# Where the first layer of the experts' weights is split into bfloat16 parts

## The reference

```
x = x + ga * attention(layernorm(x) * (1 + ca) + sa)    # 16 heads of 8, rope, causal softmax
x = x + gb * experts(layernorm(x) * (1 + cb) + sb)
# experts: h = x @ Wm + bm is cut into 8 slices of 16 numbers a token; for each slice
w     = softmax(t @ expert_emb)                         # 16 experts, the best 2 are kept
hmid  = gelu(einsum('td,edi->tei', t, W1) + b1)         # 16 -> 64, for every expert
out   = sum over the best 2 of w * (hmid @ W2 + b2)     # then @ Wo + bo
```

## Time and profile before

| | us |
|---|---|
| median of three runs | 404.51 |
| the profiled execution | 403.76 |
| its span in the trace | 402.0 |
| TensorE busy | 339.3 (84%) |
| VectorE busy | 290.0 (72%) |
| ScalarE busy | 256.4 (64%) |
| GpSimd busy | 132.9 (33%) |

### The profile page before, as it was taken

The page is one execution under the profiler, slowest core; times in us unless marked ns, Lnnn a source line. Parts: engine busy times, 40 slices in busy tenths (PEclk is TensorE's granted clock), DMA queues, the critical chain, the costliest instruction groups (busy, mean ns, idle before and its releaser), DMA issues.

```text
span 402.0 us, 7268 instructions
## 1 busy us (share of the span) xinstructions
PE 339.3 (84%) x2637; PEld 158.2 (39%) x2668; DVE 290.0 (72%) x590; ACT 256.4 (64%) x297; POOL 132.9 (33%) x175
## 2 busy tenths in 40 slices
PE   3758688888877899988987899898879898879996
PEld 3424254445543444434553534334444323222123
DVE  5879868898789877875789487874769445972343
ACT  8570443435159878865349878855437997968981
POOL 6345307201421324842313024941410035532500
PEclk9988699999899999999999999999989999999999
DMA  7334214100016055520026255520014355814552
GB/s 258 109 67 71 48 35 66 29 4 0 4 40 98 24 141 138 165 59 3 27 51 98 57 137 135 141 45 4 29 30 50 90 136 142 116 17 122 134 147 70
DMA packets 27115, 31.53 MB, mean 78 GB/s; under 512 B 6780, under 2 KB 17788, under 8 KB 27068
## 3 DMA queue, kind: packets, MB, share of 16 engines
q1 hardware_dynamic: 23372, 28.57, 31.2%
q0 software_dynamic: 3456, 2.39, 2.8%
q10 hardware_dynamic: 252, 0.11, 0.2%
HBM read 3.57 MB, written 1.05 MB: 11 GB/s over the span
## 4 chain that ended last, share of the span: by engine, by line
PE 51%; DVE 21%; issue 10%; ACT 9%; DMA 3%; POOL 2%; SPq 2%; DVEq 0%; ACTq 0%; POOLq 0%
PE misc L1290 17%; PE acc L1290 16%; PE big L1290 16%; DVE mx L1028 8%; ACT ring L769 6%; PE misc L1312 2%; DVE xn L972 2%; DMA block<-qk_turned 1%; DMA tstack<-tp 1%; ACT L802 1%; SPq L492 1%; SPq L517 1%; POOL block L446 1%; DVE stats L947 1%; POOL rpow L591 1%
## 5 line engine op out<-in xcount | busy, mean ns | idle before, releaser
L769 ACT ACTIVATE ring<-big 128x1024 f32<-128x1024 f32 (+2 forms) x225 | 198.2, 929 | 99.7 <-PE big L1290 98.4
L1028 DVE TENSOR_REDUCE mx<-misc 128x1 f32<-128x512 f32 (+7 forms) x155 | 87.8, 588 | 24.2 <-PE misc L1290 22.1
L1290 PE MATMUL acc<-ring,cb 128*32 128x512 f32 x512 | 67.8, 604 | 2.6 <-DVE gm L1148 1.5
L1290 PE MATMUL big<-dense,block 128*128 128x448 bf16 (+7 forms) x249 | 54.3, 318 | 7.4 <-ACT ring L769 7.1
L1290 PE MATMUL big<-tstack,w1s 128*128 128x512 bf16 x178 | 52.4, 381 | 5.6 <-ACT ring L769 3.9
L1290 PE MATMUL misc<-dense,block 128*128 128x320 bf16 (+7 forms) x167 | 42.0, 313 | 8.9 <-DVE mx L1028 8.6
L1148 DVE SCALAR_TENSOR_TENSOR gm<-acc,cb,gm 128x512 f32<-128x512 f32 (+1 forms) x41 | 30.0, 733 | 22.7 <-DMA gm<-wT 12.2
L1290 PEld LDWEIGHTS big<-dense,block 128*128 128x128 bf16 x256 | 30.8, 149 | 33.7 <-ACT ring L769 19.0
L446 POOL DMA_DIRECT2D block<-qk_turned x66 | 39.3, 601 | 7.9 <-DMA tstack<-tp 7.0
L670 POOL TENSOR_TENSOR gm<-osb,gm 128x512 f32<-128x512 f32 x12 | 15.8, 1316 | 76.4 <-ACT osb L809 76.4
L1290 PE MATMUL acc<-ring,vals 128*32 128x64 f32 (+7 forms) x512 | 40.7, 421 | 0.4
(11 more groups left out here) (163 smaller groups left out, 472.0 us busy)
## 6 DMA issues: line engine op xcount, KB each, us to landing
gm<-wT SPq DMA_DIRECT2D x64, 256.0 KB
dense<-qk SPq DMA_DIRECT2D x42, 64.0 KB
tstack<-tp SPq DMA_DIRECT2D x18, 128.0 KB, 4.3
block<-qk_turned POOLq DMA_DIRECT2D x66, 32.0 KB, 3.2
xs<-in_x SPq DMA_DIRECT2D x4, 256.0 KB, 8.1
ca<-in_pack_a SPq DMA_DIRECT2D x1, 769.0 KB, 7.3
out<-lg SPq DMA_DIRECT2D x3, 256.0 KB, 2.3
dense<-tp SPq DMA_DIRECT2D x6, 128.0 KB, 8.9
```

Of the source, the lines that this page charges most:

```text
L769: act.activation(dst, src, func, scale=scale).then_inc(s["ring_read"], 1)
L1028: dve.tensor_reduce(mx[:, g, k:k + n, blk], src, AX.X, ALU.max).then_inc(s["misc_read"], 1)
L1290: return pe.matmul(dst, lhsT, rhs, start=start, stop=stop)
```

## The change

VectorE's four parts are gone, and CUT_AT with them. ScalarE does the two casts, right behind take_gates. GpSimd does what was one scalar_tensor_tensor as two instructions: it multiplies w1p by the row mask into combT (a float32 tensor of 128x1024 that is free until the first experts stage), and adds that to w1f. The first pair stands behind k_blocks(0), the second behind k_blocks(1). ScalarE's second cast waits for GpSimd's first pair (w1_less at 2), GpSimd's pairs wait for the casts (w1_rounded).

```diff
-FOLD_AT, CUT_AT = [12, 15], [18, 21, 24, 27]
+FOLD_AT = [12, 15]
@@ gpsimd
+            def cut_weights(k):
+                pool.wait_ge(s["b_loaded"], 16)
+                pool.wait_ge(s["w1_rounded"], k + 1)
+                less = B["keep"][:, k:k + 1].to_broadcast([P, NE * FI])
+                rounded = combT[:].rearrange("p k t -> p (k t)")
+                pool.tensor_tensor(rounded, w1p, less, ALU.mult).then_inc(s["w1_less"], 1)
+                pool.wait_ge(s["w1_less"], 2 * k + 1)
+                if k:
+                    pool.tensor_tensor(w1s[:, :], rounded, w1f, ALU.add).then_inc(s["w1_ready"], 1)
+                else:
+                    pool.tensor_tensor(w1f, rounded, w1f, ALU.add).then_inc(s["w1_less"], 1)
...
             k_blocks(0, K_BLOCKS)
+            cut_weights(0)
             pool.wait_ge(s["spare_cleared"], 2)
             stack_q(1)
             pool.wait_ge(s["qk_turned"], 6)
             stack_k(1)
             k_blocks(1, K_BLOCKS)
+            cut_weights(1)
@@ scalar
+            def round_weights(k):
+                if k:
+                    act.wait_ge(s["w1_less"], 2)
+                else:
+                    act.wait_ge(s["w1_loaded"], 16)
+                act.copy(w1p, w1f).then_inc(s["w1_rounded"], 1)
...
             take_gates()
+            round_weights(0)
+            round_weights(1)
             act.wait_ge(s["cleared"], 3)
             shift_rows(act, 0, 0, range(1, 2))
             turn(1)
@@ vector
-            def cut_weights(part):
-                dve.wait_ge(s["b_loaded"], 16)
-                dve.wait_ge(s["w1_loaded"], 16)
-                less1, less2 = B["keep"][:, 0:1], B["keep"][:, 1:2]
-                if part == 0:
-                    link(dve.tensor_copy(w1p, w1f))
-                elif part == 1:
-                    link(dve.scalar_tensor_tensor(out=w1f, in0=w1p, scalar=less1, in1=w1f, op0=ALU.mult, op1=ALU.add))
-                elif part == 2:
-                    link(dve.tensor_copy(w1p, w1f))
-                else:
-                    dve.scalar_tensor_tensor(out=w1s[:, :], in0=w1p, scalar=less2, in1=w1f,
-                                             op0=ALU.mult, op1=ALU.add).then_inc(s["w1_ready"], 1)
...
-                if k in CUT_AT:
-                    cut_weights(CUT_AT.index(k))
```

More of the change, by code:

```diff
@@ L354, in build @@
             "gates_filled", "setup_link", "modb_ready", "w1_ready", "summed", "rows_cleared", "tokens_one",
-            "var_ready", "pow_ready", "xn_ready", "out_gates", "expert_gates", "xb_ready", "x1b_ready",
+            "var_ready", "pow_ready", "xn_ready", "out_gates", "w1_rounded", "w1_less", "expert_gates", "xb_ready", "x1b_ready",
             "misc_filled", "misc_read", "ring_filled", "ring_read", "consumed", "acc_read",
```

## The result

| | kernel before | changed kernel |
|---|---|---|
| median of 18 runs, us | 404.88 | 408.23 |
| lowest to highest, us | 401.61 to 406.45 | 404.48 to 409.99 |
| ratio, 95% interval | 1 | 1.0078 (1.005 to 1.0106) |
| profiled execution, us (span) | 403.76 (402.0) | 407.54 (405.7) |

The account below looks back on a forecast made before the run. TensorE and VectorE were taken to pace each other around the edit. +3.15 (VectorE held) - 0.6 (last multiply-add) + 1.0 (clock) = +3.5 us gave 407.3 profiled, 408.0 us as median; range 403.6 to 410.4.

Parts of the forecast that it names:

- VectorE's jobs, 0.6 of 4.1 us on the path: Of four removed VectorE instructions, only the last multiply-add (83.55 to 84.83) delays TensorE; gain about 0.6 us.
- ScalarE's casts free: Casts at 29.1 to 30.1 and until about 42.0 us cost nothing, ending 0.7 us before ScalarE's DMAs at 42.68.
- GpSimd's length, 2.5 us: Each of the four new GpSimd instructions of 128x1024 takes 2.5 us, range 2.2 to 3.3.
- The stall, 3.15 us: GpSimd's second pair, from 67.9 us, holds VectorE's second fold of the gates, which ends 3.15 us later.
- TensorE's idle time, 4.1 us: TensorE waits for maxima behind the second fold, until 74.9 us: 1.00 + 3.15 = 4.1 us.
- The clock, +1.0 us: Granted clock falls 1.4 us into TensorE's new wait, stays low 6.4 us, slowing 3.7 us of work: +1.0 us.
- The sum: Whole kernel: +3.15 held fold, -0.6 last multiply-add gone, +1.0 lower clock, together +3.5 us.
- no meeting: Second fold or GpSimd's second pair lies elsewhere by 2 us: -0.6, 403.9 us; chance 0.12.
- only the first fold instruction is held: In the second fold, GpSimd's addition comes too late to hold more: +1.0 - 0.6, no clock loss, 404.9 us; chance 0.14.
- all 4.1 us come back: VectorE is the bound in 60 to 86 us, so its removed work is fully regained: 401.0 us; chance 0.10.
- the slow GpSimd: GpSimd needs 3.3 us per instruction, delaying ScalarE by 0.9 us and VectorE more: +6.0, 410.5 us; chance 0.10.

Follow-up runs that it names:

- the first experiment: Changed kernel with GpSimd's second pair moved behind stack_q(1), before the wait for element 1's turned queries: 404.16 us, ratio 1.0008 to the kernel before.

## Why the prediction was right

The kind of cause was right: the second pair and the fold of the gates hold each other, TensorE stands still for it, and the clock falls. Which fold is held, and by how much each term weighs, was partly wrong, and the errors nearly cancel.

- *VectorE's jobs, 0.6 of 4.1 us on the path.* Measured 0.56: the distance falls from 3.69 to 3.12 between 76.5 and 88.4. The size is right, its place only in part. By TensorE's instructions 0.16 had come back ahead of the last multiply-add (81.17 and 84.70 are 3.53 apart). At its place TensorE gains 0.75 (85.42 and 88.20, 2.78) and loses 0.36 of that two units later, in the wait of 0.52 before 90.15 (87.01 and 90.15, 3.14). So the jobs counted as free were not quite free, and the wait of 0.59 came back for 0.39.
- *ScalarE's casts free.* They took 1.08 and 1.04 us; the second ended at 41.34 and the DMAs went out at 43.08, 1.7 us later. Right, with more cover than the 0.7 us feared.
- *GpSimd's length, 2.5 us.* The multiplication of bfloat16 took 1.91, the addition 2.36: a pair is 0.7 us shorter than taken. The multiplication passed the bound of 2.2 us from below; it has a bfloat16 input and a broadcast column, which no row had shown, and no run tells which of the two, or the operation itself, makes it shorter.
- *The stall, 3.15 us.* 3.04 us measured (2.69 on L945 and 0.03 on L944 of the first fold, 0.32 on L943 of the second), but not where the step put it. The step failed on the first fold: it took 67.86, the end of the DMA issues, as the moment from which VectorE can be held, and so let L920 (67.09 to 67.78) pass. In the changed kernel GpSimd's last wait ahead of the pair was passed at 67.36, with two DMA issues still to run, and L945, issued at 67.59, was held until the multiplication's end at 70.40. The second fold then came when most of the addition was over, and lost 0.32 us rather than 3.15. That the two agree in sum is partly luck: with the first fold kept clear by a wait, the predicted pattern appears, and holds 2.5 us. The row that would have shown it was in the trace before: L1050, 0.28 us long at its shortest, issued at 169.28 and held until 171.58, while GpSimd's L682 is recorded only from 170.15.
- *TensorE's idle time, 4.1 us.* 3.95 us, but it is another wait: the step added 3.15 to the 1.00 behind the second fold, and measured were 1.22 + 2.73 behind the first. Again the sum agrees by luck.
- *The clock, +1.0 us.* It fell, but not 1.4 us into the wait and for 6.4 us, as the step had it: it fell at the wait's end and stayed low for 3.4 us, all of it behind the wait. The step had come to 3.7 us behind the wait, so this too agrees by luck. That work took longer: TensorE's distance grows from 3.18 (68.43 and 71.61) to 4.36 us (70.33 and 74.68), and then falls back to 3.69. From 71.61 to 76.65 TensorE needed 5.04 us for what took 4.53 from 68.43 to 72.96 before, though the 4.53 contain the second fold's wait of 1.00 us, and only 0.15 is left of it, since the slower TensorE no longer runs ahead of VectorE. The net is +0.5 us. The term was mis-sized: the step gave the full price of slow matmuls and did not take off the wait that they cover.
- *The sum.* +2.73 (growth of the first wait) + 0.51 (from there to 76.65, clock and second fold together) - 0.56 = +2.68 us, against +2.67 by the same instructions at the end of that softmax. The prediction had +3.5. The medians give 3.35 us, 0.7 more than this pair of profiles; what lies between is within the interval of the ratio, and no run here explains it.

Of the rivals, "no meeting" fell with the profile; "only the first fold instruction is held" had the shape nearly right (one instruction carries 2.69 of the 3.04 us) and its price of 1.0 us wrong; "all 4.1 us come back" fell with the first experiment, ratio 1.0008 with the stall removed; the slow GpSimd fell with 1.91 us. What the prediction did not see is that, once the split was gone, the place of the fold was worth more than the split: from 404.16 to 402.28 us, by the profiles 0.56 us gained with the fold in its old place (and no stall) and 1.70 with the late one.

What stays open: whether VectorE is held from the moment that the GpSimd instruction is handed over, or GpSimd's recorded starts are late. Three places show the same 0.8 to 0.9 us between the two (169.28, 67.59, and 68.00 with the pair added). The run with the added wait speaks for the first: there the multiplication cannot have started before 67.40 and is recorded from 67.63, so a recorded start was late by at most 0.23 us. That it was no later at the three places is argued from this one run, not measured there.

## What to carry to other kernels

Moving elementwise work from VectorE to GpSimd gives VectorE back only what was on the path, here 0.6 of 4 us, and it can hold VectorE for the length of the GpSimd instruction: lay the new GpSimd instructions over VectorE's timeline, and keep them beside instructions that were not held, such as reductions out of PSUM. Count from where GpSimd's last wait ahead of the instruction is passed, here 1.0 to 1.3 us before its recorded start, and look again at what GpSimd does next when the order changes. Before moving a job to another engine, try another order of the jobs on its own: here that alone gave a ratio of 0.9971 (0.9946 to 0.9996), with 0.29 us to show for it in the profile, and with the move it gave 0.9954, the best of all.

## What the runs showed of the hardware

- A GpSimd multiplication of 128x1024 with a bfloat16 input and a broadcast mask column took 1.91 us, an addition of two float32 tensors of that size 2.36 us.
- Held beside GpSimd arithmetic: scalar_tensor_tensor on two SBUF tensors (0.69 to 3.38 us), tensor_scalar (0.43 to 2.45), a cast of 32x128 (0.21 to 1.26). Beside memsets only the tensor_scalar. Maxima out of PSUM: not, beside either; the 155 in the page's group have a mean of 588 ns before and after.
- An instruction that is let in between two of the other engine delays the second one: the addition took 2.69 us in place of 2.36.
- A GpSimd instruction held VectorE from before its recorded start: by 0.91 us with its waits passed 1.14 us ahead of that start, and not at all where its wait was passed only 0.23 us ahead.
